# One batch in sixteen goes to its bucket row by row instead of packed

## What is computed

```python
edge_aggr = zeros((6250, 128)).at[src].add(edge_attr_128)      # sum of edge rows by source node
combined = concat([x, edge_aggr, global_expand], -1) @ W_c + b_c
h = softplus(combined @ W1 + b1)
h = softplus(h @ W2 + b2)
out = layernorm(x + h @ W3 + b3)
```

## Time and profile before

| | |
|---|---|
| time, median of 3 runs | 1839.99 us (1839.88 to 1840.54) |
| time of the profiled execution | 1839.51 us |
| its span on the core | 1837.8 us |
| mean granted TensorE clock | 0.983 of full speed |
| busy: PE / DVE / ACT / POOL | 1755.9 / 1377.6 / 1104.6 / 1177.6 us |
| stage of moves and scatters, from the first bucket end to the last | 93.5 to 1298.8 us |

### The profile page before, as it was taken

How to read it: one execution, slowest core, us unless ns; L and a number is a source line. 1 busy time by engine, 2 the same in 40 slices (tenths; PEclk the granted TensorE clock), 3 DMA queues, 4 the chain that set the end, 5 groups by cost and what they waited for, 6 DMA issues and landing times.

```text
span 1837.8 us, 63834 instructions
## 1 busy us (share of the span) xinstructions
PE 1755.9 (96%) x15333; PEld 1686.4 (92%) x15333; DVE 1377.6 (75%) x3909; ACT 1104.6 (60%) x3526; POOL 1177.6 (64%) x1477
## 2 busy tenths in 40 slices
PE   7899999999999999999999999999599999999975
PEld 4799989999999999999999999999599999999942
DVE  7877767777777777777777777777478888888846
ACT  1455455455555555555555555555378888888877
POOL 1577777777777777777777777777545554454424
PEclk9899999999999999999999999999799999999998
DMA  6388888877777777777777777777589999999902
GB/s 154 111 266 251 244 238 256 252 236 223 218 225 217 226 212 224 217 222 219 218 221 211 228 212 223 217 224 214 191 282 293 283 286 283 283 283 285 283 22 59
DMA packets 349556, 414.12 MB, mean 225 GB/s; under 512 B 28544, under 2 KB 249776, under 8 KB 347996
## 3 DMA queue, kind: packets, MB, share of 16 engines
q1 hardware_dynamic: 284003, 233.87, 44.9%
q0 software_dynamic: 57840, 176.38, 29.4%
q10 hardware_dynamic: 7689, 3.60, 1.0%
HBM read 233.69 MB, written 180.02 MB: 225 GB/s over the span
## 4 chain that ended last, share of the span: by engine, by line
PE 67%; issue 8%; POOLq 7%; POOL 7%; ACT 3%; DMA 3%; SPq 1%; DVE 0%; ACTq 0%; DVEq 0%
PE ps L1074 58%; POOL sums L519 6%; POOLq L514 5%; PE ps L1148 4%; DMA buckets<-arena,index 2%; PE ps L1041 2%; PE ps L1047 2%; POOL buckets L486 1%; PE ps L1045 1%; ACT arena L939 1%; POOLq L518 1%; ACT arena L942 1%; ACT arena L940 1%; POOLq L519 1%; POOLq L516 1%
## 5 line engine op out<-in xcount | busy, mean ns | idle before, releaser
L1074 PE MATMUL ps<-arena 128*120 (+1 forms) x9672 | 1171.1, 279 | 0.8 <-DVE arena L707 0.3
L1074 PEld LDWEIGHTS ps<-arena 128*120 128x120 f32 x9672 | 1124.0, 184 | 1.4 <-issue 1.1
L486 POOL DMA_INDIRECT buckets<-arena,index x806 | 845.3, 1049 | 272.0 <-issue 226.8
L707 DVE TENSOR_SCALAR arena<-slot_no,slot_f 128x360 f32<-128x360 f16 x1612 | 607.5, 420 | 308.9 <-PE ps L1074 285.7
L888 ACT ACTIVATE arena<-ps 120x387 f32<-120x387 f32 x806 | 397.6, 493 | 564.0 <-PE ps L1074 498.7
L1148 PE MATMUL ps<-mark,members 128*128 128x128 f32 x3648 | 426.6, 279 | 21.2 <-ACT mark L971 21.2
L1148 PEld LDWEIGHTS ps<-mark,members 128*128 128x128 f32 x3648 | 419.7, 194 | 28.1 <-issue 21.4
L756 DVE TENSOR_SCALAR mark<-node_no,members 128x128 f32<-128x128 f16 x1368 | 363.3, 326 | 75.4 <-DMA members<-buckets 38.7
L519 POOL TENSOR_TENSOR sums<-sums,staged 128x128 f32 x456 | 213.8, 469 | 228.4 <-ACT staged L959 210.0
L854 ACT ACTIVATE reach<-block_no,arena 128x120 f16<-128x120 f16 x806 | 310.3, 386 | 0.6 <-PE ps L1084 0.6
L965 ACT ACTIVATE apart<-node_no,members 128x128 f32<-128x128 f16 x456 | 180.3, 395 | 30.7 <-DMA members<-buckets 23.3
(11 more groups left out here) (148 smaller groups left out, 606.4 us busy)
## 6 DMA issues: line engine op xcount, KB each, us to landing
members<-buckets SPq DMA_DIRECT2D x456, 258.0 KB, 3.3
arena<-in_feats SPq DMA_DIRECT2D x201, 512.0 KB
buckets<-arena,index POOLq DMA_INDIRECT x806
arena<-in_xT SPq DMA_DIRECT2D x12, 250.0 KB, 5.6
xn<-in_x ACTq DMA_DIRECT2D x1, 2800.0 KB
out_rows<-xn SPq DMA_DIRECT2D x12, 224.0 KB
arena<-in_src SPq DMA_DIRECT2D x1, 805.5 KB
buckets<-sums,end_now POOLq DMA_INDIRECT x50
```

Source lines behind the costliest of these rows:

```text
L486: pool.indirect_dma_start(units, bass.IndirectOffsetOnAxis(ap=index[0:SLOTS, s, b:b + 1], axis=0), rows[0:SLOTS, o, :], None).then_inc(sca ...
L707: dve.tensor_scalar(perm[0:TP, b, t, :], slot_no[0:TP, :, :].rearrange("p r b -> p (r b)"), slot_f[0:TP, s % 2, b * TPB + t:b * TPB + t + ...
L1074: mm = pe.matmul(ps[0:SLOTS, MOVED + b, r * ROWF:(r + 1) * ROWF], perm[0:TP, b, t, r * SLOTS:(r + 1) * SLOTS], feat[0:TP, bass.ds(at, 1), ...
```

## The change

The last batch of each body (number 15, `is_direct`) isn't permuted, moved and taken any more. Its rank comes out as the absolute place: PE adds two small matmuls with the place of the batch's first row in each bucket (`first_hi`, `first_lo`, made once by DVE in `firsts`). DVE multiplies it (`direct_at`), and POOL issues two indirect DMAs of 128 single rows straight from `feat` (`scatter_direct`). Stream 7 then has one packed batch in a body in place of two. Who reuses what the direct DMAs read or follow waits for `direct_landed`: SP's load into slot 3, ACT's `set_locals` for slot 3, `take_rows` of stream 7, DVE's next `direct_at`. `packed(i, k)` counts the batches that are moved. The places of the bucket end and of the spare tiles are no longer copied by POOL but by ACT, after the fifth batch of the body (`take_end`, `take_spare`). PE's loop has 16 batches of code where two nested loops had 8.

```diff
+        def packed(i, k):
+            return i * (BODY - 1) + (k - k // BODY)
+        def is_direct(k):
+            return k % BODY == BODY - 1
...
+            def reload(i, s):
+                if s == XS - 1:
+                    sp.wait_ge(direct_landed, i * (16 * TPB))
+                else:
+                    sp.wait_ge(moved, packed(i, (s + 1 - XS) * CB))
+                load(i * XS + s, s, i * (XS // 2) + s // 2)
...
             def end_of_bucket(i):
-                wait(pool, ends_zeroed, i * 16)
-                pool.tensor_copy(end_now[:, :], end_at[:, bass.ds(i, 1)]).then_inc(end_taken, 1)
                 pool.wait_ge(end_taken, i + 1)
...
+            def scatter_direct(i):
+                pool.wait_ge(direct_ready, i + 1)
+                pool.wait_ge(scattered[STREAMS - 1], i * 16 + 32)
+                if not isinstance(i, int):
+                    pool.nop(nofuse=True)
+                for t in range(TPB):
+                    pool.indirect_dma_start(
+                        units, bass.IndirectOffsetOnAxis(ap=direct_at[0:TP, t:t + 1], axis=0),
+                        feat[0:TP, XS - 1, (CB - 1) * TPB + t, :], None).then_inc(direct_landed, 16)
...
             def scatter_body(i):
-                for s in range(XS):
-                    for b in range(CB):
-                        scatter(i * BODY + (s * CB + b), i * XS + s, s, b)
+                for k in range(BODY - 1):
+                    scatter(i, k)
+                scatter_direct(i)
...
+            def permutation(i, k):
...
+                if is_direct(k):
+                    turn = i + k // BODY
+                    wait(dve, direct_landed, turn * (16 * TPB))
+                    dve.tensor_scalar(direct_at[0:TP, :], slot_f[0:TP, s, b * TPB:(b + 1) * TPB], float(RUNITS), None,
+                                      ALU.mult).then_inc(direct_ready, 1)
+                    return
...
-            def set_locals(c, s):
-                wait(act, moved, (c + 1 - XS) * CB)
+            def set_locals(i, s):
+                c = i * XS + s
+                if s % XS == XS - 1:
+                    wait(act, direct_landed, (i + s // XS) * (16 * TPB))
+                else:
+                    wait(act, moved, packed(i, (s + 1 - XS) * CB))
...
+            def take_end(i):
+                wait(act, ends_zeroed, i * 16)
+                if not isinstance(i, int):
+                    act.nop(nofuse=True)
+                act.activation(end_now[:, :], end_at[:, bass.ds(i, 1)], ACT.Copy).then_inc(end_taken, 1)
...
+            with act.Fori(1, SPARES) as i:
+                for k in range(BODY):
+                    take(i, k)
+                    if k == CB:
+                        take_spare(i)
+                        take_end(i)
...
+                if s == XS - 1:
+                    body = i
+                    pe.wait_ge(firsts_made, 2)
+                    for part, table in ((first_hi, ident128_16[0:K, :]), (first_lo, ident2_16[0:K, 0, :])):
+                        pe.matmul(out_[:, CB - 1, :, :], part[0:K, bass.ds(body, 1)].to_broadcast([K, TP]),
+                                  table.unsqueeze(1).to_broadcast([K, TPB, K]), start=False, stop=False)
...
+            def work(i, k):
+                last = isinstance(i, int)
+                if k % CB == 1 and (not last or k // CB + 2 < CHUNKS):
+                    rank(i, k // CB + 2)
+                if not is_direct(k):
+                    move(i, k)
+                if not last or k + RS < NBAT:
+                    goto(i, k + RS)
```

More of the change, by code:

```diff
@@ L860, in indices @@
                 if not isinstance(c, int) or c >= XS:
-                    for b in range(CB):
+                    for b in range(CB - s % 2):
                         act.wait_ge(scattered[s % 2 * CB + b], turn * 16)
+                    if s == 1:
+                        act.wait_ge(scattered[STREAMS - 1], 16 + body * 16)
                 act.activation(index[0:SLOTS, s, 0:n], ps[0:SLOTS, GOTO + s % 2, 0:n], ACT.Identity,
@@ L879, in set_locals, with take_rows @@
                     act.nop(nofuse=True)
[L880 removed]
+                act.activation(feat[0:TP, s % XS, 0:n, D], local1[0:TP, bass.ds(c * (CB * TPB), n)], ACT.Copy)\
                    .then_inc(locals_set, 1)
[L883 to L888 removed]
+            def take_rows(i, k):
+                o, turn = k % STREAMS, i * (BODY // STREAMS) + k // STREAMS
+                act.wait_ge(moved, packed(i, k + 1))
+                if o == STREAMS - 1:
+                    body = i + k // BODY
+                    wait(act, direct_landed, body * (16 * TPB))
+                    wait(act, scattered[o], body * 16 + 16)
+                elif not isinstance(i, int) or turn:
+                    act.wait_ge(scattered[o], turn * 16 + 16)
+                act.activation(rows[0:SLOTS, o, :], ps[0:SLOTS, MOVED + k % CB, 0:BLK], ACT.Copy).then_inc(rows_ready, 1)
@@ L890, in _, with take @@
             act.wait_ge(local_a, 2)
             for c in range(XS - 1):
-                set_locals(c, c)
+                set_locals(0, c)
             for g in range(RS, AHEAD):
                 reached(g, g % RS)
-            indices(0, 0, 0)
-            def take(g, b, c, s, turn):
-                ends = isinstance(g, int)
+            indices(0, 0, 0, 0)
+            def take(i, k):
+                ends = isinstance(i, int)
+                s, b = k // CB, k % CB
+                c = i * XS + s
@@ L899, in take @@
                 if b == 0 and (not ends or c + XS - 1 < CHUNKS):
-                    set_locals(c + (XS - 1), (s + XS - 1) % XS)
+                    set_locals(i, s + (XS - 1))
                 if b == 1 and (not ends or c + 1 < CHUNKS):
-                    indices(c + 1, (s + 1) % XS, turn + (s % 2 + 1) // 2)
-                take_rows(g, b, s, turn)
-                if not ends or g + AHEAD < NBAT:
-                    reached(g + AHEAD, (s * CB + b + AHEAD) % RS)
-            def take_body(i):
-                for s in range(XS):
-                    for b in range(CB):
-                        take(i * BODY + (s * CB + b), b, i * XS + s, s, i * (XS // 2) + s // 2)
@@ L912, in _ @@
-            take_body(0)
-            with act.Fori(1, BODIES - 1) as i:
-                take_body(i)
+                    indices(c + 1, (s + 1) % XS, i * (XS // 2) + (s + 1) // 2, i + (s + 1) // XS)
+                if not is_direct(k):
+                    take_rows(i, k)
+                if not ends or k + AHEAD < NBAT:
+                    reached(i * BODY + (k + AHEAD), (k + AHEAD) % RS)
+            for k in range(BODY):
+                take(0, k)
+            act.wait_ge(end_at_made, 2)
@@ L915, in _ @@
+            take_spare(0)
+            take_end(0)
+            with act.Fori(1, SPARES) as i:
+                for k in range(BODY):
+                    take(i, k)
+                    if k == CB:
+                        take_spare(i)
+                        take_end(i)
+            with act.Fori(SPARES, BODIES - 1) as i:
+                for k in range(BODY):
+                    take(i, k)
+                    if k == CB:
+                        take_end(i)
             for g in range((BODIES - 1) * BODY, NBAT):
-                take(g, g % CB, g // CB, g // CB % XS, g // STREAMS)
+                take(0, g)
+                if g == (BODIES - 1) * BODY + CB:
+                    take_end(BODIES - 1)
```

166 lines of the change are left out of this document (89 added, 77 removed).

## The result

The changed kernel takes 1937.07 us (median of 4 runs, 1934.01 to 1941.65), the kernel before 1839.93 (1839.55 to 1840.54). The ratio is 1.053, with an interval of 1.0508 to 1.0552: slower, by 97 us. The profiled execution took 1941.65 us with a span of 1940.0, 102.1 us more than that of before.

What follows compares the result with a forecast made beforehand. PE bounds the kernel, except the first bodies, where POOL does; after the change a POOL-ACT loop does. 1839.5 + 74 (drain) + 18 (POOL's stalls) + 16 (ACT's copies) = 1947.5 us, likeliest 1947, range 1885 to 2010.

Steps and rivals of the forecast that it cites:

- the drain: At each body's start ACT waits for POOL's direct DMAs, emptying the pipeline 49 times: 26.1 us a body, +74 us.
- (a): POOL's recurring standstills with input ready, formerly free, now cost time: some 8 of 2.25 us, +18 us.
- (b): ACT's copies at the fifth batch wait for earlier DMAs in 11 bodies with spare tiles: 1.5 us each, +16 us.
- rival 1: PE's pauses also bring half clock after each drain: 0.7 to 1.0 us a body, 42 us, about 1990; chance 0.17.
- the landing: Time from the second direct DMA's end until ACT goes on: 2.2 us, range 1.7 to 3.2.
- POOL's step: One packed scatter costs POOL 1.34 us, fifteen times in a body's period.
- PE is 1.0 us ahead, so it isn't the bound: After a drain PE has batch 14's rows ready 17.8 us after the first scatter; POOL wants them at 18.8.
- PE's pause in the long part: PE stands 3.1 us in each body; its busy share there falls from 99.8% to below 90%.
- POOL's gap: POOL's first scatter of each body comes after a gap of 2 us or more.
- ACT's wait: ACT's first instruction of a body waits some 4 to 6 us, 49 times, 200 to 300 us in total.
- its 24.0: POOL's own work in a body of the changed kernel without a spare: 24.0 us, above PE's 23.0.

Runs made afterwards that it cites:

- e1: Changed kernel with ACT setting local numbers two chunks ahead instead of three, so its wait stands four batches later: 1867.3 us, ratio 1.0146.
- e3: Changed kernel with ACT's local numbers set two chunks ahead and its copies of the places moved to after the 13th batch: 1835.04 us, ratio 0.9975.
- e8: Changed kernel with ACT's setting of local numbers, and its wait, one batch later, at a chunk's second batch: 1883.29 us, ratio 1.0252.
- e4: Changed kernel plus 14 useless matmuls a body on PE, behind the move of batch 3: 1913.21 us, ratio 1.0406.
- e2: Changed kernel with ACT's copies of the places after the 13th batch of a body instead of the fifth: 1918.74 us, ratio 1.0437.
- e12: Changed kernel with SP's load of slot 3 held until six batches of the next body have moved: 1916.42 us, ratio 1.042.
- e5: Kernel before, with ACT instead of POOL copying the places, after the fifth batch, and no direct batch: 1816.79 us, ratio 0.9881.
- e6: Kernel before, with ACT instead of POOL copying the places, after the 13th batch, and no direct batch: 1816.34 us, ratio 0.9879.

## Why the prediction was right, and where it was mis-sized

The forecast was slower, at 1947 (1885 to 2010); it came out slower, at 1937. That the number is so near is in part luck: the drain was put 39 us too high, and the clock, which the main sum left out, cost some 30. The mechanism of the drain is what the runs show. The sum's terms against what they measured, on the stage's 95.4 us:

| term | forecast | measured |
|---|---|---|
| drain, PE not the bound | +74 | +35 |
| (a) POOL's stalls | +18 | about +10 |
| (b) ACT's copies in spare bodies | +16 | +13 to +18, 2 to 6 of it clock |
| clock (only in rival 1) | 0, or +42 | about +30 |

The measured terms overlap and come from different runs, so they add up to 88 to 93 and not to 95.4.

**The drain is right in mechanism, twice too large.** A body without stall or half clock takes 25.31 us, from one bucket end to the next (792.0 to 817.3, below), so 49 x (25.31 - 24.6) = 35. Forecast were 26.1. Of the 0.8 us, 0.69 is the landing: 1.51 us, where I took 2.2 from a row of 2.3 at the end of the stage. The range reached down to 1.7, so the landing lies outside it. The ends of the range, 1885 and 2010, don't quite follow from its terms either: added up, these give 1889 to 2024. The rest is POOL's step, 1.33 us in place of 1.34, fifteen times. That the wait's place is the cause is shown by e1, e3 and e8: the later it stands, the shorter the body of the long part, with the same wait and the same DMAs.

**"PE is 1.0 us ahead, so it isn't the bound" failed.** It holds at full clock only, and even there PE needs 23.5 us a body (e3), not 23.0, so it was less than 1.0 ahead. The two stretches below are the two neighbouring bodies, 27 and 28, of the changed kernel, and one inside the second; PE's pause at the start of the first is the next row.

```profile
792.00:817.30 25.30, 23.61 (x217) 22.81 (x216) 17.11 (x44) 12.67 (x40) 18.36 (x18) 1.00 0.71 209
817.30:844.00 26.70, 25.02 (x215) 23.90 (x214) 17.00 (x44) 12.79 (x40) 18.32 (x19) 0.94 0.68 198
```

```profile
794.34 0.21 PE L1189 MATMUL ps<-goto,reach 128*120 x1 [1.67 <-ACT reach L910]
```

```profile
819.90:823.30 3.40, 3.40 (x19) 2.76 (x20) 0.77 (x3) 2.78 (x11) 2.59 (x3) 0.57 0.99 273
```

Both bodies have a pause of 1.67 us at the same place; behind the second the granted clock falls from the level of 2.4 GHz to that of 1.2 GHz for about 3.4 us, and the body takes 26.7 us. Half clock comes in 22 of the 49 bodies, 7 of them with spare tiles. By the stretches above the half clock adds up to 0.06 x 306 / 0.5 + 0.03 x 994 / 0.5 = 96 us; the clock's own records have 92, before 3.4. Most bodies with it take about 1.35 us more than those without; for 22 that is 30 us, an estimate. e4 bears it out by filling the pause: half clock 20.5 us, time 24 less. Rival 1 was thus partly true, 30 of its 42. The Trainium skill, page "TensorE: Matmul & The Clock Gate", section "HAM oscillation — how this bites in real kernels", says of a kernel whose pauses are waits of about 3 to 5 us that PE is throttled again in each tile. Here the pauses are mostly shorter, half clock came in 22 of 49 bodies, and identical pauses fall on both sides.

PE's pause in the long part was mostly 1.4 to 2 us (half of them up to 1.7), forecast 3.1, and its busy share 92.8%, forecast below 90%. Of the 1.4 us between 3.1 and 1.7, 0.8 is the shorter body; the rest is that PE is busy 23.6 us in a body at full clock, where I had 23.0. At half clock the stretched matmuls count as busy too. POOL's gap was 1.77 us in the body shown, forecast 2 or more. ACT's wait, 290.3 us in 49 times, was as forecast.

**(a)** came in bodies 5, 23, 34 and 45, four times and not eight; the last three are 11 bodies or 198 indirect DMAs apart, where before it was 102. One of them:

```profile
708.55 0.99 POOL L507 DMA_INDIRECT buckets<-arena,index  x1 [2.37 <-issue]
```

They don't fall into the drain: the body with the stall is 2.3 to 2.7 us longer, and PE's pause in the next is 3.5 to 4.1 us instead of 1.7, with half clock behind it. The four together are about 10 us. The cause of the stalls stays open: they are absent from e3 and from e1's long part, with the same 18 indirect DMAs a body. It is not a refetch of a longer PE loop: the instruction queue moved 10 packets in all.

**(b)** was right in size: in the first 11 bodies 17.6 us by e2 and 12.9 by e12. Both hold some clock, since half clock falls from 34 to 17 us there in e2 and from 24 to 17 in e12. The cause given for it was right too, as far as e12 goes: SP's load of slot 3, held until the direct batch has landed, runs beside the spare's and the bucket end's bytes, and holding it back takes the wait from 35.9 to 9.5 us. They don't stand in one queue: SP's loads are on q1 of the page, POOL's indirect DMAs on q0. How the one slows the other isn't shown. What I hadn't seen is that the wait at the fifth batch costs nothing without the direct batch (e5).

**The copies and POOL.** I counted the copies' departure from POOL as part of its 24.0 and saw no gain of its own; alone it is worth 1.2% (e6), of which 13.4 us lie in the stage. The direct batch on top of it frees 0.8 us of PE in a body of the long part (24.27 in e6, 893.34 / 38 = 23.5 in e3) and asks 1.2 more of POOL, which then bounds the body at 24.04 (e3). With both waits placed well that makes the stage less than 2 us longer than in e6; the 18.7 us between the two kernels lie mostly behind it. So the copies alone gain 23 us, and the whole change loses 97: the direct batch, as its waits are placed, turns the one into the other.

Of the 5.8 us behind the stage, 4.7 are POOL's last instruction, before and after (duration in ns, start in us):

```profile
L88 POOLq DRAIN  x1: 5030/5030/5030, 1832.5 to 1832.5; - x1
```

```profile
L89 POOLq DRAIN  x1: 9683/9683/9683, 1930.0 to 1930.0; - x1
```

It takes 9.68 us in each kernel with the direct batch, and 5.03 in e5, e6 and the kernel before. What it waits for the profile doesn't show. e3's end, too, is 3.9 us longer than that of before.

## What to carry to other kernels

When an instruction at the head of an in-order queue waits for a DMA that is issued behind that queue's own output, two engines empty each other; put the wait where the other engine has stock, here four batches later for 70 us. Count for an engine what it costs per instruction from start to start: POOL read 64% busy and had 0.9 us to spare in a body, and the cheap half of this change, taking a copy of 0.7 us a body off it, was the half worth having. When two variants differ, look where: most of what parts e3 from e6 lies behind the stage that they change. When PE gets a pause, price the clock too, as a chance for each pause, and test it with useless matmuls.

## What the hardware did that was not expected

- Two pauses of PE of the same 1.67 us (before 794.34 and before 819.64) had different consequences: clock 1.00 in one body, 0.57 for 3.4 us in the next. In e8 the pauses of the long part were mostly 0.5 us, and half clock there 10 us; in the changed kernel it was 58.
- 132 KB of direct rows were waited for only 1.51 us after POOL had issued the second DMA; the page's median for them from issue to landing is 2.3 us, and 3.7 for a scatter. Over the 49 bodies it was 1.35 to 1.8 us.
- POOL stood still for 2.4 to 3.2 us with its input ready once in 198 indirect DMAs, before once in 102, in e3 never.
- The stage behind, with the same 456 loads, took 418 us in the two kernels with the copies alone on ACT, and 427 to 429 in all others. POOL's last instruction took 9.68 us in the kernels with the direct batch and 5.03 in those without.
- One chip ran the kernel before in 2099 us, 14% above the others; the ratio of the same changed kernel was nearly the same on both (1.0396 and 1.042).
